# Second attention: the value matmuls of a pair of steps, cut into two halves of 256 queries

## The reference

```
qkv = x @ Wqkv + bqkv                      # 16 query heads, 4 heads of keys and values, 16 wide
scores = einsum('bqhd,bkhd->bhqk', q, k) / HD
prob = softmax(scores)
out = einsum('bhqk,bkhd->bqhd', prob, v) @ Wout + bout
```

## Time and profile before

| | |
|---|---|
| median of 3 runs | 2173.84 us (2172.9 to 2176.99) |
| profiled execution | 2171.24 us, span 2169.1 us |
| PE busy over the span | 2093.0 us (96%) |
| DVE, ACT busy | 1452.7 us (67%), 1211.7 us (56%) |
| second attention, first score to last copy | 1324.4 to 1677.7 us |

### The profile page before, as it was taken

How to read it: one execution, slowest core, us unless ns; L and a number is a source line. 1 busy time by engine, 2 the same in 40 slices (tenths; PEclk the granted TensorE clock), 3 DMA queues, 4 the chain that set the end, 5 groups by cost and what they waited for, 6 DMA issues and landing times. The chain is left out here.

```text
span 2169.1 us, 31294 instructions
## 1 busy us (share of the span) xinstructions
PE 2093.0 (96%) x11136; PEld 1596.3 (74%) x11136; DVE 1452.7 (67%) x2761; ACT 1211.7 (56%) x2435; POOL 577.9 (27%) x679
## 2 busy tenths in 40 slices
PE   7999999999999999989999989999998899999997
PEld 6888888888888888877788863333333678778886
DVE  5666666667666776666656568888883556655555
ACT  5666666666556666644444444777777434444343
POOL 3444444444334444422222210000000112222221
PEclk9999999999999999999999996999999999999999
DMA  2000000000000000011111120000000111111111
GB/s 74 20 21 20 13 21 20 21 20 20 9 20 21 21 20 21 16 31 39 44 44 44 44 53 14 17 21 18 19 20 2 43 34 47 41 47 37 51 52 56
DMA packets 54301, 64.78 MB, mean 30 GB/s; under 512 B 9179, under 2 KB 34566, under 8 KB 54150
## 3 DMA queue, kind: packets, MB, share of 16 engines
q1 hardware_dynamic: 54150, 62.81, 10.6%
HBM read 52.68 MB, written 2.10 MB: 25 GB/s over the span
## 5 line engine op out<-in xcount | busy, mean ns | idle before, releaser
L861 POOL TENSOR_TENSOR a_pr<-a_pr,a_rinv 128x512 f32<-128x512 f32 (+3 forms) x384 | 312.8, 829 | 477.8 <-DVE a_rinv L1108 477.8
L86 PE MATMUL psum<-xh,g_hi_gu 128*128 128x512 f32 x928 | 377.8, 407 | 15.4 <-DVE xl L1091 9.2
L88 PE MATMUL psum<-xh,g_lo_gu 128*128 128x512 f32 x928 | 363.8, 392 | 0.0
L87 PE MATMUL psum<-xl,g_hi_gu 128*128 128x512 f32 x928 | 363.1, 391 | 0.0
L1782 DVE TENSOR_REDUCE a_negm<-psum 128x1 f32<-128x1024 f32 x256 | 301.5, 1220 | 36.3 <-PE psum L1660 35.5
L1189 POOL TENSOR_TENSOR g_lo_gu<-g_raw_gu,g_hi_gu 128x512 fp32r<-128x512 f32 x84 | 108.9, 1296 | 796.2 <-ACT g_hi_gu L1185 796.2
L1763 ACT ACTIVATE a_pt<-psum 128x512 f32<-128x512 f32 x512 | 268.2, 603 | 81.4 <-PE psum L1675 81.1
L1483 DVE TENSOR_TENSOR f_hl<-f_hid,f_hh 128x512 fp32r<-128x512 f32 x168 | 116.9, 696 | 238.2 <-ACT f_hh L1421 236.3
L1410 ACT ACTIVATE f_act_s<-psum,g_gu_bias 128x512 f32<-128x512 f32 x168 | 115.0, 685 | 276.4 <-PE psum L88 276.1
L1013 ACT ACTIVATE a_pr<-psum,a_negm 128x128 f32<-128x128 f32 (+7 forms) x256 | 190.3, 743 | 106.7 <-DVE a_negm L1098 102.7
L1020 ACT ACTIVATE a_pth<-psum 128x512 fp32r<-128x512 f32 (+3 forms) x384 | 174.8, 490 | 113.2 <-PE psum L920 109.6
(11 more groups left out here) (290 smaller groups left out, 4307.5 us busy)
## 6 DMA issues: line engine op xcount, KB each, us to landing
g_raw_gu<-in_gu SPq DMA_DIRECT2D x84, 256.0 KB, 2.8
f_raw_dn<-in_down SPq DMA_DIRECT2D x84, 128.0 KB, 2.0
g_raw_gu<-in_qkv SPq DMA_DIRECT2D x32, 256.0 KB, 2.8
a_wvr<-in_qkv SPq DMA_DIRECT2D x32, 128.0 KB, 2.4
a_wor<-in_o SPq DMA_DIRECT2D x32, 128.0 KB, 2.1
x_queries_qq<-x_qhi SPq DMA_DIRECT2D x128, 32.0 KB, 2.0
yT<-in_xT SPq DMA_DIRECT2D x4, 512.0 KB, 6.4
x_queries_qq<-x_qlo SPq DMA_DIRECT2D x64, 32.0 KB, 1.9
```

The source lines that it names most:

```text
L86: pe.matmul(out, a_hi, b_hi, start=first, stop=False)
L87: pe.matmul(out, a_hi, b_lo, start=False, stop=False)
L88: return pe.matmul(out, a_lo, b_hi, start=False, stop=last)
L861: pool.tensor_tensor(x, x, rinv[:, j:j + 1].to_broadcast([P, count * P]), ALU.mult).then_inc(p_done, 1)
```

## The change

`values` gets a second argument. Half 0 covers the first 256 queries of the chunk and carries the waits; half 1 covers the other 256 and carries the increment of `pv_done`. The first half is issued at the head of an even step, ahead of its maxima and scores, the second at the head of the odd step. Before, all of it was issued in the odd step between its last maxima matmul and its last score.

```
-            def values(n):
+            def values(n, half):
...
+                x = slice(half * CH // 2, (half + 1) * CH // 2)
+                if half == 0:
+                    pe.wait_ge(exp_done, (n + 1) * G1)
+                if kt == 0 and half == 0 and u >= 1:
...
                 for g in range(G1):
+                    m = pe.matmul(acc_ps[g * W:(g + 1) * W, x], vs[b][:, kt, g, :], pt[:, n % SLOTS, g, x],
+                                  start=kt + half == 0, stop=kt + half == NK, tile_position=(0, g * W))
+                if half == 1:
+                    m.then_inc(pv_done, 1)
...
                 for i in range(STEPS):
+                    if u * NK + i // 2 >= LAG:
+                        values(u * NK + i // 2 - LAG, i % 2)
                     ahead = maxima_at(u, i)
...
                         if ahead:
                             maxima(*ahead, k, bank)
-                        if k == 1 and i % 2 == 1 and u * NK + i // 2 >= LAG:
-                            values(u * NK + i // 2 - LAG)
                         scores(u, i, k)
...
             for n in range(LAG):
-                values((LAST + 1) * NK - LAG + n)
+                for half in range(2):
+                    values((LAST + 1) * NK - LAG + n, half)
```

More of the change, by code:

```diff
@@ L1676, in scores @@
                           qq[p0:p0 + ROWS + 1, u % QSLOT, g % 2, :], start=True, stop=True).then_inc(st_ready, 1)
-            def values(n):
+            def values(n, half):
                 u, kt = n // NK, n % NK
                 b, j, c = UNITS[u]
-                pe.wait_ge(exp_done, (n + 1) * G1)
-                if kt == 0 and u >= 1:
+                x = slice(half * CH // 2, (half + 1) * CH // 2)
+                if half == 0:
+                    pe.wait_ge(exp_done, (n + 1) * G1)
+                if kt == 0 and half == 0 and u >= 1:
                     pe.wait_ge(zt_done, u)
                 for g in range(G1):
-                    m = pe.matmul(acc_ps[g * W:(g + 1) * W, :], vs[b][:, kt, g, :], pt[:, n % SLOTS, g, :],
-                                  start=kt == 0, stop=kt == NK - 1, tile_position=(0, g * W))
-                m.then_inc(pv_done, 1)
+                    m = pe.matmul(acc_ps[g * W:(g + 1) * W, x], vs[b][:, kt, g, :], pt[:, n % SLOTS, g, x],
+                                  start=kt + half == 0, stop=kt + half == NK, tile_position=(0, g * W))
+                if half == 1:
+                    m.then_inc(pv_done, 1)
             def turn(u, with_z, with_m, bank):
```

## The result

The changed kernel takes 2268.65 us (median of 4 runs, 2241.66 to 2270.85), the kernel before 2173.37 beside it: a ratio of 1.041, interval 1.036 to 1.046. The forecast was 2176. It missed by 93 us, and in the direction that the first rival had named.

What follows compares the result with a forecast made beforehand. The prediction took a ring of scores, exponentials and whole values in the second attention as the bound. Per unit, 1.20 us gained against the new wait and turn left 0.11 more, 1.7 in all: 2176 us, range 2163 to 2198.

Steps and rivals of the forecast that it cites:

- the first rival: Second attention: granted clock falls to 0.50 in the new wait, 1.5 us lost per fall, 2187 to 2199 us; chance 0.26.
- The ring goes: Second attention: scores no longer stand behind values that follow another score's wait, a loop of 2.61 us a pair.
- A step of 1.23, with 0.57 for half the values: On PE, load to load: 0.66 for maxima and scores plus 0.57, sixteen steps making 19.68 us a unit.
- The cut has no price: On PE: the values' weight loads overlap, so the skill's matmul overhead, 0.2 us a pair, is not added.
- the last rival: On PE: each added matmul has its own price, 0.10 us a pair, 0.8 a unit, 2189 us; chance 0.12.
- The stall of 1.55: Head of step 4 in 15 units: PE stands 1.55 us while a unit's first values wait for ACT's copy.
- The turn, 0.85: A unit's transposes on PE: 0.70 us plus an estimated 0.15 for a slot not yet free.
- A unit of 22.08: Second attention: 19.68 for steps, 1.55 for the wait and 0.85 for the turn, against 21.97 us before.
- The sum of 2176: Whole kernel: 0.11 us more a unit, 1.7 us over 15 units, from the median of 2173.84; chance 0.50.

Runs made afterwards that it cites:

- the cut alone: Kernel before, with the values of a pair in two halves back to back at the old place: 2184.16 us, ratio 1.001.
- the single stalls: Changed kernel with ACT's copy ahead of step 3's exponentials, except in three units that keep the late copy: ratio 1.002 to the kernel before.
- the filled wait: Changed kernel with six maxima matmuls run on PE in the wait at the fifth step of each unit from the second on: 2204.9 us, ratio 1.014.
- the early copy: Changed kernel with ACT's copy of the finished sums ahead of step 3's two exponentials instead of behind them: 2162.14 us, ratio 0.991.
- the later turn: Changed kernel with the transposes of the turn three steps later, at a unit's thirteenth step instead of the tenth: 2275.79 us, ratio 1.043.
- the burst: Changed kernel with six more maxima matmuls at the head of each unit's seventh step from the second unit on: 2317.06 us, ratio 1.066.
- mixed pairs: Changed kernel with only each unit's first pair in halves, the other pairs as whole values at the old place: 2232.03 us, ratio 1.019.

## Why the prediction was wrong

- *The ring goes*: right. 110.6 us of waiting in 293 us of the stage became 8.1 in 393.
- *A step of 1.23, with 0.57 for half the values*: right to the last digit shown, in the two steps in a row above at full clock; 0.57 from a half's first load to the next one is in the rows below.
- *The cut has no price* (and with it the last rival): right, 22.00 against 21.97 a unit with the cut alone.
- *The stall of 1.55*: right. 1377.06 to 1379.86 is 2.80, less a step of 1.23 is 1.57.
- *The turn, 0.85*: right. The values on both sides of it load at 1688.79 and 1690.87, 2.08 apart, which is 1.23 + 0.85.
- *A unit of 22.08*: right where the clock held. The undisturbed unit's copies lie at 1681.89 and 1704.02, 22.13.

The rows of the step and of the last two points, of the kernel after: values around a turn, and ACT's copies of the undisturbed unit.

```profile
1688.79 0.16 PEld L1688 LDWEIGHTS psum<-a_pt,x_vs 128*32 128x32 f32 x8 [0.36 <-issue]
1689.36 0.18 PEld L1660 LDWEIGHTS psum<-x_ks,x_queries_qq 48*128 48x128 f32 x1 [0.41 <-DVE a_negm L1786]
...
1690.87 0.16 PEld L1688 LDWEIGHTS psum<-a_pt,x_vs 128*32 128x32 f32 x8 [0.22 <-issue]
```

```profile
1681.89 0.60 ACT L1754 ACTIVATE a_zt<-psum 128x512 f32<-128x512 f32 x1
...
1704.02 0.60 ACT L1754 ACTIVATE a_zt<-psum 128x512 f32<-128x512 f32 x1
```

And the point that failed:

- *The clock falls in the new wait*: the mechanism that I had as a rival with a chance of 0.26 is what happened. The sum of 2176 held nothing for it, and the price that the rival gave it failed too: "A stretch of 3.3 us as in the earlier trace rows holds 1.5 steps in place of 2.7, which loses 1.5 us". The stretches were 6.8 to 17.1 us and 75.1 at the end, the loss 3 to 7 us each and 32, together 100 in place of 15 x 1.5 = 22. I took the stretch's length from 543.4 to 546.7, from another stage. The same group held a row of this very stage, 40.8 us at 0.50 with PE busy 35.9 of them: there PE at work had not brought the clock back soon. That row should have set the upper end. Even 13 stretches of 7 us, a sixth of it, would, at 0.43 lost of each microsecond, have put the rival's time at 2215 (the 13 and the 7 are known only now), beyond the range's end. Of the 100 us, the 32 of the last stretch lie in the steps without maxima, where the cut alone fell to 0.50 without such a stall; so it isn't shown that all of the 32 come from the stall ahead of it.
- Its chance was too low as well. I weighed a gap of 1.55 over which the clock held. That row was a sample of one, and the single stalls show that one is not enough: the same gap held twice and fell once in one run.

Shown by runs: with the standing still shortened to 0.30 or 0.57, or filled with work, the clock, once at 1.00, stays there through the units of the same stream. Shown too: a stall of 2.04 in the old stream, or of 1.26 in one close to it, lowers it part of the time. Not settled: which stalls lower it, and what sets the length of a stretch.

## What to carry over

A change that evens out waits can gather them into one gap on TensorE, and the price of the gap is then not its length but the stretch at 1.2 GHz that may follow. Take the upper end of that stretch from the longest one in the same stage, not from the shortest anywhere, and don't take its chance from one row: here the same stall lowered the clock in 13 of 14 units of one kernel and in 1 of 3 of another. Before such a change, move what the gap waits for: one copy taken two exponentials earlier turned a loss of 4% into a gain of 0.6 to 0.9%.

## What the runs showed of the hardware

The granted clock stayed at 0.50 while PE worked with hardly a gap in the rows: 13.60 of 13.60 us in the changed kernel, 134.36 of 139.9 with the filled wait. The same kinds of instruction ran at 1.00 for 304 us on end with the early copy. The Trainium skill, "TensorE: Matmul & The Clock Gate", Part 1, has the clock return after sustained activity. These rows don't agree, as far as activity is what the rows call busy.

Whether a stall lowers the clock was not a matter of its length alone: in the profiled runs 0.30 and 0.57 never did, 1.26 did in 11 of 14 units, 1.53 in 13 of 14 in the changed kernel, 12 of 14 with the later turn, 12 of 13 with the burst and 1 of 3 where it came alone, 2.04 in 5 of 14. The same section says that the activity meter runs on its own and doesn't start with the kernel. That one of three identical stalls fell, and that runs of one program lie 29 us apart (the changed kernel) and 53 (mixed pairs), agree with it and do not prove it.
